# Expert ranks of a routed decoder layer: the running counts ride in row 0 of the choices, one product instead of two

## The reference

```
xf = _layernorm(x.reshape(-1, Dd), ln_g, ln_b)
logits = xf @ router_w
scores, idx = jax.lax.top_k(logits, K)          # K = 2 of E = 8
gate = jax.nn.softmax(scores, axis=-1)
gates_e = jnp.zeros((N, E)).at[jnp.arange(N)[:, None], idx].add(gate)
out = sum over experts e of gates_e[:, e] * expert_e(xf)
```

## Time and profile before

| | us |
|---|---|
| median of 3 runs | 626.74 |
| lowest, highest | 625.05, 631.46 |
| the profiled execution: time | 622.47 |
| the profiled execution: span | 620.7 |
| PE busy in the span | 564.1 |
| VectorE busy | 491.7 |
| ScalarE busy | 427.9 |
| GpSimd busy | 385.3 |

### The profile page before, as it was taken

How to read it: one execution, slowest core, us unless ns; L and a number is a source line. 1 busy time by engine, 2 the same in 40 slices (tenths; PEclk the granted TensorE clock), 3 DMA queues, 4 the chain that set the end, 5 groups by cost and what they waited for, 6 DMA issues and landing times.

```text
span 620.7 us, 18226 instructions
## 1 busy us (share of the span) xinstructions
PE 564.1 (91%) x5212; PEld 448.2 (72%) x5212; DVE 491.7 (79%) x1516; ACT 427.9 (69%) x1179; POOL 385.3 (62%) x747
## 2 busy tenths in 40 slices
PE   3598999999999999999999788897999999999495
PEld 2265677777777777777676677786799888888395
DVE  1367898888989888898999677889988888888443
ACT  2266888888888888888877665545466666665235
POOL 2474558787878888787877755665354443443344
PEclk9999999999999999999998999999999999999889
DMA  3471211313113131121110454554566666666183
GB/s 98 128 102 42 72 41 39 89 44 84 51 47 87 41 90 41 54 81 50 49 41 12 137 154 130 173 176 150 154 192 196 200 195 193 197 201 188 48 305 95
DMA packets 68914, 69.29 MB, mean 112 GB/s; under 512 B 7072, under 2 KB 50144, under 8 KB 68816
## 3 DMA queue, kind: packets, MB, share of 16 engines
q1 hardware_dynamic: 62880, 56.81, 31.7%
q0 software_dynamic: 5168, 10.55, 5.6%
q10 hardware_dynamic: 768, 0.75, 0.4%
HBM read 53.38 MB, written 14.71 MB: 110 GB/s over the span
## 4 chain that ended last, share of the span: by engine, by line
PE 71%; DVE 10%; DMA 6%; issue 5%; ACT 4%; SPq 1%; POOL 1%; ACTq 0%; POOLq 0%; DVEq 0%
PE ps_s L735 11%; PE ps_t L746 10%; PE ps_a L757 6%; PE ps_m L807 6%; PE ps_a L766 4%; PE ps_s L787 4%; DVE hid L1421 4%; PE ps_s L789 3%; PE ps_t L787 3%; PE ps_t L789 3%; ACT sil L1051 3%; PE ps_m L663 2%; DMA w1t<-in_L_ffn_W_dram 2%; PE ps_m L719 2%; PE ps_m L630 1%
## 5 line engine op out<-in xcount | busy, mean ns | idle before, releaser
L1145 DVE TENSOR_TENSOR sc<-ps_s,decay 128x512 f32<-128x512 f32 x128 | 84.8, 685 | 27.2 <-PE ps_s L735 26.9
L520 POOL DMA_INDIRECT expert_out<-yt,dest x71 | 71.0, 1000 | 42.9 <-issue 23.8
L807 PEld LDWEIGHTS ps_m<-wot,hid 128*128 128x128 f32 x568 | 83.3, 191 | 19.0 <-DVE hid L1425 8.8
L807 PE MATMUL ps_m<-wot,hid 128*128 128x128 f32 x568 | 90.4, 278 | 6.3 <-DVE yt L1432 3.5
L735 PE MATMUL ps_s<-kbd,qT 32*128 32x512 f32 x256 | 75.9, 670 | 10.1 <-DMA kbd<-key_image 6.0
L901 ACT ACTIVATE pT<-ps_t 128x512 f32<-128x512 f32 x128 | 72.6, 592 | 16.3 <-PE ps_t L746 16.3
L746 PEld LDWEIGHTS ps_t<-ident,sc 128*128 128x128 f32 x512 | 58.0, 145 | 32.2 <-issue 30.6
L1156 DVE TENSOR_REDUCE rowmax<-sc 128x8 f32<-128x1024 f32 x64 | 78.1, 1220 | 0.4
L986 ACT ACTIVATE sc<-sc,rowmax 128x128 f32<-128x128 f32 x256 | 77.9, 390 | 0.0
L746 PE MATMUL ps_t<-ident,sc 128*128 128x128 f32 x512 | 77.7, 286 | 0.0
L491 POOL DMA_INDIRECT expert_in<-xhat,pos x64 | 65.2, 1018 | 16.5 <-issue 14.0
(11 more groups left out here) (275 smaller groups left out, 1437.2 us busy)
## 6 DMA issues: line engine op xcount, KB each, us to landing
w2t<-in_L_ffn_W_dram SPq DMA_DIRECT2D x39, 256.0 KB
w1t<-in_L_ffn_W_dram SPq DMA_DIRECT2D x39, 256.0 KB
wot<-in_L_ffn_Wo_dram SPq DMA_DIRECT2D x39, 256.0 KB, 3.8
kbd<-key_image SPq DMA_DIRECT2D x32, 256.0 KB
xst<-expert_in SPq DMA_DIRECT2D x32, 130.0 KB, 2.1
g<-expert_out SPq DMA_DIRECT2D x7, 512.0 KB, 8.4
key_image<-kT SPq DMA_DIRECT2D x32, 64.0 KB, 2.0
call<-in_ctx_dram SPq DMA_DIRECT2D x8, 256.0 KB, 6.7
```

The source lines that it names most:

```text
L520: pool.indirect_dma_start(ys_dram[:, :], bass.IndirectOffsetOnAxis(ap=dest[:, n, a:a + 1], axis=0), yt[:, par, a, :], None).then_inc(y_out ...
L807: mm = pe.matmul(ps_y(i)[:, a * P:(a + 1) * P], hid[:, par, c, a * P:(a + 1) * P], wot[:, par, c, :], start=(c == 0 and a == 0), stop=(c = ...
L1145: dve.tensor_tensor(sc[:, 2 * (b % 2) + i // 2, j:j + 4, :], ps_s[:, i % 2, :, :], decay[:, :].unsqueeze(1).to_broadcast([P, 4, S]), ALU.m ...
```

## The change

`cum` is gone. A row of 8 numbers, `base_row`, holds the running counts, and each batch's `both` gets it as its row 0, in place of row 0's own choices. The matrix `earlier` now counts the rows after a row instead of those before it, and its row 0 is all ones, so that one product gives every row the running counts plus the choices of the rows after it. Row 0's own choices are kept aside in `own0`, and VectorE adds them to row 0 of the product to make the next `base_row`: row 0 of the product is the running counts plus the choices of rows 1 to 127. The tables read the counts with `first`, a matrix whose row 0 is ones and the rest zeros. A last `total` replaces the last `count`.

```
@@ constants
-                pool.iota(iota_i[:, c + 2 + E:c + 2 + 2 * E], pattern=[[N // P, E]], base=0,
+                pool.iota(iota_i[:, c + 2 + E:c + 2 + 2 * E], pattern=[[N, E]], base=0,
                           channel_multiplier=0).then_inc(rcst, 1)
                 pool.affine_select(out=earlier[:, :], in_=ones[:, :], compare_op=ALU.is_ge, fill=0.0,
-                                   base=-1, pattern=[[1, P]], channel_multiplier=-1).then_inc(rcst, 1)
+                                   base=-1, pattern=[[-1, P]], channel_multiplier=1).then_inc(rcst, 1)
-                pool.tensor_copy(cum[:, :], iota_i[:, B + 2 + E:B + 2 + 2 * E]).then_inc(rcst, 1)
+                pool.tensor_copy(base_row[:, :], iota_i[0:1, B + 2 + E:B + 2 + 2 * E]).then_inc(rcst, 1)
+                pool.memset(first[:, :], 0.0).then_inc(rcst, 1)
+                pool.wait_ge(rcst, 17)
+                pool.memset(first[0:1, :], 1.0).then_inc(rcst, 1)
+                pool.memset(earlier[0:1, :], 1.0).then_inc(rcst, 1)
@@ GpSimd
                 def choices(b):
                     pool.wait_ge(oh_ready, b + 1)
                     before(pool, ranked, b)
+                    pool.tensor_tensor(both[:, :], oh[:, b % 2, 0, :], oh[:, b % 2, 1, :], ALU.add).then_inc(chosen, 1)
+                    before(pool, cum_ready, b - 1)
+                    pool.tensor_tensor(own0[:, b % 2, :], oh[0:1, b % 2, 0, :], oh[0:1, b % 2, 1, :], ALU.add)
+                    pool.wait_ge(chosen, b + 1)
                     before(pool, cum_ready, b)
-                    pool.tensor_tensor(both[:, :], oh[:, b % 2, 0, :], oh[:, b % 2, 1, :], ALU.add).then_inc(both_ready, 1)
+                    pool.tensor_copy(both[0:1, :], base_row[:, :]).then_inc(both_ready, 1)
-                def count(b):
-                    pool.wait_ge(ranked, b + 1)
-                    pool.wait_ge(both_ready, b + 1)
-                    pool.tensor_tensor(cum[:, :], cum[:, :], both[:, :], ALU.add).then_inc(cum_ready, 1)
+                def total():
+                    pool.wait_ge(ranked, B)
+                    pool.wait_ge(cum_ready, B)
+                    pool.tensor_copy(both[0:1, :], base_row[:, :]).then_inc(both_ready, 1)
@@ TensorE, ranks(b)
-                    before(pe, cum_ready, b)
                     if b == EARLY:
-                        pe.matmul(m2e, ones[:, :], cum[:, :], start=True, stop=True)
-                    pe.matmul(m2d, earlier[:, :], both[:, :], start=True, stop=False)
-                    pe.matmul(m2d, ones[:, :], cum[:, :], start=False, stop=True).then_inc(ranked, 1)
+                        pe.matmul(m2e, first[:, :], both[:, :], start=True, stop=True)
+                    pe.matmul(m2d, earlier[:, :], both[:, :], start=True, stop=True).then_inc(ranked, 1)
@@ TensorE, all_counts
-                    pe.wait_ge(cum_ready, B)
+                    pe.wait_ge(both_ready, B + 1)
                     pe.wait_ge(rank_read, B)
-                    pe.matmul(m2e, ones[:, :], cum[:, :], start=True, stop=True).then_inc(rt_cnt, 1)
+                    pe.matmul(m2e, first[:, :], both[:, :], start=True, stop=True).then_inc(rt_cnt, 1)
@@ VectorE, own_rank(b)
                     before(dve, row_ready, b - 1)
+                    dve.tensor_tensor(base_row[:, :], m2d[0:1, :], own0[:, b % 2, :], ALU.add).then_inc(cum_ready, 1)
                     dve.tensor_tensor(rnk[:, b % 2, :, :], oh[:, b % 2, :, :],
                                       m2d.unsqueeze(1).to_broadcast([P, 2, E]), ALU.mult).then_inc(rank_read, 1)
```

More of the change, by code:

```diff
@@ L94, in decoder_layer @@
         ones = sb("ones", [P, P])
-        earlier = sb("earlier", [P, P])
+        earlier = sb("earlier", [P, P]); first = sb("first", [P, P])
         decay = sb("decay", [P, P])
@@ L146, in decoder_layer @@
         both = sb("both", [P, E])
-        cum = sb("cum", [P, E])
+        base_row = sb("base_row", [1, E]); own0 = sb("own0", [1, 2, E])
         rnk = sb("rnk", [P, 2, 2, E])
@@ L189, in decoder_layer @@
         top_ready = sem("top_ready"); logits_read = sem("logits_read"); oh_ready = sem("oh_ready")
-        both_ready = sem("both_ready"); ranked = sem("ranked"); cum_ready = sem("cum_ready")
+        both_ready = sem("both_ready"); ranked = sem("ranked"); cum_ready = sem("cum_ready"); chosen = sem("chosen")
         rank_read = sem("rank_read"); row_ready = sem("row_ready"); pos_ready = sem("pos_ready"); tagged = sem("tagged")
@@ L408, in _ @@
                 pool.memset(line[:, 1, :, E + 1:E + 2], float((E - 1) * N)).then_inc(line_ends, 1)
-                pool.tensor_copy(cum[:, :], iota_i[:, B + 2 + E:B + 2 + 2 * E]).then_inc(rcst, 1)
+                pool.tensor_copy(base_row[:, :], iota_i[0:1, B + 2 + E:B + 2 + 2 * E]).then_inc(rcst, 1)
                 pool.tensor_copy(thr[:, :], iota_i[:, c:c + 2 * MAXT]).then_inc(rcst, 1)
                 pool.tensor_copy(tile_no[:, :], iota_i[:, c + 2 * MAXT:c + 2 * MAXT + TILES]).then_inc(rcst, 1)
-                pool.wait_ge(rcst, 16)
+                pool.memset(first[:, :], 0.0).then_inc(rcst, 1)
+                pool.wait_ge(rcst, 17)
+                pool.memset(first[0:1, :], 1.0).then_inc(rcst, 1)
+                pool.memset(earlier[0:1, :], 1.0).then_inc(rcst, 1)
+                pool.wait_ge(rcst, 19)
                 def rstd1_of(b):
@@ L529, in beside @@
                     if (i, place_) == (1, 2): rstd4_of(B - 3); biased_sum(B - 1)
-                    if (i, place_) == (2, 0): rstd2_of(B - 2); count(B - 5)
+                    if (i, place_) == (2, 0): rstd2_of(B - 2)
                     if (i, place_) == (2, 2): router_rows(B - 2); place(B - 5); scatter(B - 5)
@@ L533, in beside @@
                     if (i, place_) == (4, 2): rstd4_of(B - 2)
-                    if (i, place_) == (5, 0): rstd2_of(B - 1); count(B - 4)
+                    if (i, place_) == (5, 0): rstd2_of(B - 1)
                     if (i, place_) == (5, 1): router_rows(B - 1)
@@ L537, in beside @@
                     if (i, place_) == (6, 1): rstd4_of(B - 1)
-                    if (i, place_) == (6, 2): count(B - 3)
                     if (i, place_) == (7, 1): choices(B - 2); tag(B - 2); place(B - 3)
-                    if (i, place_) == (7, 2): scatter(B - 3); count(B - 2)
+                    if (i, place_) == (7, 2): scatter(B - 3)
                     if (i, place_) == (8, 1): choices(B - 1); tag(B - 1); place(B - 2)
                     if (i, place_) == (8, 2): scatter(B - 2)
-                    if (i, place_) == (9, 0): count(B - 1)
+                    if (i, place_) == (9, 0): total()
                     if (i, place_) == (9, 2): place(B - 1); scatter(B - 1)
@@ L552, in _ @@
                     if ever(s - 7): scatter(s - 7)
-                    if ever(s - 6): count(s - 6)
                     if ever(s - 2): biased_sum(s - 2)
@@ L703, in ranks @@
                     if b == 0:
-                        pe.wait_ge(rcst, 16)
+                        pe.wait_ge(rcst, 19)
                     if b >= B - 5:
                         upto(pe, oT_ready, b + 3)
-                    before(pe, cum_ready, b)
                     if b == EARLY:
-                        pe.matmul(m2e, ones[:, :], cum[:, :], start=True, stop=True)
-                    pe.matmul(m2d, earlier[:, :], both[:, :], start=True, stop=False)
-                    pe.matmul(m2d, ones[:, :], cum[:, :], start=False, stop=True).then_inc(ranked, 1)
+                        pe.matmul(m2e, first[:, :], both[:, :], start=True, stop=True)
+                    pe.matmul(m2d, earlier[:, :], both[:, :], start=True, stop=True).then_inc(ranked, 1)
                 def second_sum(s):
@@ L1259, in one_hot @@
                     if b == 0:
-                        dve.wait_ge(rcst, 16)
+                        dve.wait_ge(rcst, 19)
                     dve.tensor_tensor(oh[:, b % 2, :, :], iota_e[:, :].unsqueeze(1).to_broadcast([P, 2, E]),
```

## The result

| | before | changed |
|---|---|---|
| median of 20 runs, us | 626.82 | 621.32 |
| lowest, highest | 622.48, 631.46 | 616.95, 625.73 |
| profiled execution: span | 620.7 | 618.8 |

The account below looks back on a forecast made before the run. PE was taken to bound batches 0 to 21, with VectorE sharing the chain later. 5.94 us for PE's product, less 0.4 for VectorE and 0 for the tail, gave 5.5 off 626.74: 621.2 us, range 617 to 626.

Parts of the forecast that it names:

- PE's product: Line 712 on PE goes once per batch: 0.22 us in each of batches 0 to 26, 5.94 us gained.
- The argument from batch 23: Batch 23 has a third product and takes 1.12 us against 0.90, so one product less should save 0.22.
- The rival in which the product was nearly free: On PE, weights load beside other work, only streaming counts: 0.05 us gained per batch, 625.8 us; chance 0.08.
- GpSimd's delay: Two operations behind `both` delay GpSimd by 0.32 us (0.40 at most), hidden by ScalarE's 0.72 us of slack.
- The rival of GpSimd as the bound: Operations and waits behind `both` fill GpSimd's loop: gain shrinks from 0.80 us added, 633.3 us at 1.25; chance 0.05.
- VectorE's new operation: Addition to `own0`, 0.10 us: hidden in batches 0 to 22, costs 0.4 us (0.3 to 0.6) in 23 to 26.
- The tail: Five batches ranked between expert tiles: taken as 0, bounds 0.4 us gained and 0.5 lost.
- the rival on PE's clock: One more fall of PE's clock loses 1.7 us, 622.9 (chance 0.08); the existing one going gives 619.5 (0.05).
- The sum: Whole kernel: 5.94 - 0.4 - 0 = 5.5 us off the median of 626.74, giving 621.2 us, 0.9% less.
- The forecast's range of 5.0 to 6.2 us: Range of the whole gain, said to come from the bounds of the forecast's terms.

Follow-up runs that it names:

- product_back: Changed kernel with a second product of the same shape put back ahead of the product in every batch; 0.9996 of the kernel before, second chip.
- two_more_b: Changed kernel with two more unused one-partition additions on GpSimd behind `both` in each batch, third chip; 1.0101 of the kernel before.
- two_more_one_input_b: Changed kernel with two more GpSimd additions per batch and the `nm` step taking one SBUF tensor and a scalar column, third chip; 0.9929 of the kernel before.
- place_late: Changed kernel with GpSimd's two table entries behind the big subtraction instead of ahead of it, second chip; 0.9917 of the kernel before.
- one_input_b: Changed kernel with the `nm` step taking one SBUF tensor and a scalar column, third chip; 0.9935 of the kernel before.
- one_input: Changed kernel with the `nm` step taking one SBUF tensor and a scalar column, first chip; 1.0005 of the kernel before.
- two_more_one_input: Changed kernel with two more GpSimd additions per batch and the `nm` step taking one SBUF tensor and a scalar column, first chip; 1.0005 of the kernel before.

## Why the prediction was right

**PE's product: right.** 0.22 us on the chain, and putting it back takes all of the gain. The argument from batch 23, that a third product lengthened the batch by 0.22, held for the removal too. The rival in which the product was nearly free is out: it gave 625.8. It went by the price of a matmul in the Trainium skill, "VectorE: DVE Perf Modes", section on the TRN2 errata, and the trace disagrees with 0.22 us on the chain.

**What PE kept of it: slightly off.** 0.186 per batch in batches 0 to 22, so 4.1 us over these 22 batches instead of 4.8. The forecast had checked GpSimd's delay against ScalarE's exponential (0.72 us of slack) and PE's need of `both`. It named the right delay and the wrong waiter. The first to feel it was VectorE's `nm` step, which waits for no semaphore of the subtraction. Before the change, on the second chip, the step began almost exactly when the subtraction ended, by luck:

```profile
199.32 1.89 POOL L440 TENSOR_TENSOR sc<-sc,rowmax 128x1024 f32<-128x1024 f32 x1
...
201.17 0.14 DVE L1182 SCALAR_TENSOR_TENSOR nm<-mv,rs 128x1 f32<-128x1 f32 x1
```

The subtraction ends at 201.21, 0.04 us after the step's start. From there the later lengths can be added up: with GpSimd 0.30 us later, 0.34 us (product_back showed 0.34); with PE's second sum also 0.22 us earlier, 0.56 us (the changed kernel showed 0.56). This kernel had no slack at that place, and the change used up 0.42 us of VectorE's time per batch. The rival of GpSimd as the bound, with a chance of 0.05 and a threshold of 0.80 us, had both the path and the threshold wrong. Late GpSimd work costs time from about 0.30 us on, the delay of the change itself, and 0.30 us beyond that the kernel is slower than before (two_more_b). But GpSimd's own loop is not what was reached: with the `nm` step in its other form the same 0.6 us cost nothing (two_more_one_input_b).

**VectorE's new operation: right in price, high in effect.** 0.14 us long, the next 0.07 behind it, hidden in batches 0 to 22. For batches 23 to 26 I took 0.4 us off. The chain of the changed kernel passes through it in three of these batches, with 0.16 us in all, and once more between the expert tiles:

```profile
316.39 0.04 DVE base_row L1275
...
326.61 0.06 DVE base_row L1275
...
337.35 0.06 DVE base_row L1275
...
385.42 0.15 DVE base_row L1275
```

The starts of the product in batches 22 to 24 are 10.19 and 10.56 us apart in the second chip's run of the kernel before, and 9.99 and 10.36 us in that of the changed one: 0.20 us gained in each. Batches 25 and 26 can't be compared, since a fall of the clock lies there in three of the four profiles.

**The tail and the clock.** The tail's 0 was too good in what the profiles show. From the routing product of batch 27 to that of batch 28 it took 22.4 and 22.6 us in the two profiles of the changed kernel, against 21.2 in both of the kernel before. PE's granted clock fell there in both profiles of the changed kernel and in neither of the other. Windows of about the same tiles, changed kernel first:

```profile
376.00:381.00 5.00, 4.22 (x15) 3.42 (x16) 3.80 (x12) 1.79 (x5) 2.24 (x3) 0.66 0.43 146
```
```profile
379.00:384.00 5.00, 3.82 (x23) 3.27 (x24) 4.44 (x14) 2.52 (x7) 1.96 (x3) 1.00 0.48 167
```

That is a fall which the forecast did not count on, at 1.2 to 1.4 us, near the 1.7 of the rival on PE's clock, which had a chance of 0.08. Whether the change brings it is open: place_late and one_input_b, which contain the change, took 21.1 us there without a fall, and one_input took 23.4 with one on the first chip.

**The sum.** 5.5 us were forecast and 5.5 measured between the medians; on the second chip the medians lie 4.9 us apart. Where the profiles have it, in us gained:

| stretch | first profiles | second chip |
|---|---|---|
| up to batch 0 | -0.4 | 2.9 |
| batches 0 to 22 | 4.1 | 4.1 |
| 22 to 24 | 0.4 | 0.4 |
| 24 to 27 | -0.9 | 1.2 |
| 27 to 28 | -1.2 | -1.4 |
| 28 to the end | 0.0 | -1.1 |
| sum | 2.0 | 6.1 |

Only three rows come out alike in both: 4.1, 0.4 and a loss of 1.2 to 1.4. The others move by more than a microsecond from one pair to the next, and the falls of the clock lie in other places in each profile. So 4.5 us of the gain are located, and what makes 5.5 of them in the medians is not known. That the forecast hit 5.5 is in part luck. The forecast's range of 5.0 to 6.2 us for its terms doesn't follow from them either: their bounds give 5.94 - 0.6 - 0.5 = 4.8 to 5.94 - 0.3 + 0.4 = 6.0 us.

## What to carry to other kernels

Where the chain runs through one engine alone, the price of an instruction there is best read from a place in the same trace that has one more of it. When work is added to a half-idle engine, ask not only who waits for its results, but also which instruction elsewhere shares something with its long ones: here a step on one column, held to the end of a subtraction that it doesn't depend on. Here the step could take its second column as a scalar column instead, and was free of it, at 0.20 us instead of 0.14.

## What the runs showed of the hardware

Batch 0 is ranked at 87.4 us in the first profile of the kernel before and at 90.2 us in the second. The same code ran; in 40 to 60 us the granted clock was 1.00 in the one and 0.83, a mix of both levels, in the other:

```profile
40.00:60.00 20.00, 17.26 (x219) 12.03 (x217) 14.44 (x26) 14.52 (x43) 7.29 (x9) 1.00 0.31 64
```
```profile
40.00:60.00 20.00, 16.88 (x195) 11.95 (x197) 12.39 (x22) 11.94 (x35) 5.18 (x6) 0.83 0.28 61
```

In all 14 profiles, the four with 1.00 in this stretch ranked batch 0 at 86.5 to 87.4 us, the three with 0.83 at 90.2 to 90.3, and the seven with one short fall at 87.8 to 90.5. So the clock is not all of it, but this early stretch can cost some 3 us or nothing in executions of the same code. And chips differ: the kernel before had medians of 633.35, 628.25 and 626.15 us on the three, and on the slowest, from its batch 5 on, PE's results of a projection reached ScalarE mostly 0.7 to 1.2 us after the product's start instead of 0.50. The first batch there took 9.72 us too in one_input and two_more_one_input, before the scatters to DRAM began; whether these are the cause was not tried.
